# A hand-written order of the attention stage on one Trainium2 core: the repeated period in another order, the last group and its tail in a list of their own

## The reference

```
for gp in 4 head groups, bb in 4 batches:        # a step s = 4*gp + bb
    q, qx, k, v = quantised layernorm(x) @ weights     # row products, 256 rows
    q, qx, k    = layernorm over each head of 128
    4 heads:  softmax(q k^T) v                         # self attention, 256 x 256
    4 heads:  softmax(qx kx^T) vx                      # cross attention, 256 x 64
    y = round to fp8 (concat / smooth);  x += y @ wproj
then x = x + mixture of 32 experts(layernorm(x)), a second attention, a dense ffn
```

## Time and profile before

| | us |
|---|---|
| median of 3 runs | 820.1 (819.15 to 820.65) |
| the profiled execution | 821.01 |
| its span | 819.2 |
| PE busy in the span | 776.4 (95%) |
| PE's weight loads | 669.2 (82%) |
| DVE busy | 642.5 (78%) |
| ACT busy | 538.4 (66%) |
| POOL busy | 495.5 (60%) |
| granted TensorE clock, mean | 0.991 of full |

### The profile page before, as it was taken

How to read it: one execution, slowest core, us unless ns; L and a number is a source line. 1 busy time by engine, 2 the same in 40 slices (tenths; PEclk the granted TensorE clock), 3 DMA queues, 4 the chain that set the end, 5 groups by cost and what they waited for, 6 DMA issues and landing times.

```text
span 819.2 us, 14427 instructions
## 1 busy us (share of the span) xinstructions
PE 776.4 (95%) x4848; PEld 669.2 (82%) x4848; DVE 642.5 (78%) x1509; ACT 538.4 (66%) x1236; POOL 495.5 (60%) x858
## 2 busy tenths in 40 slices
PE   3678999999999999999899999999999999999997
PEld 2467888889888899888778878898888877777787
DVE  6878998989888898889889795766754658886644
ACT  6889878798787987788664555433332267986332
POOL 2698879997699976997856477424210125627410
PEclk9989999999999999999999999999999999999999
DMA  7000120012101030000200322977513000001001
GB/s 248 13 1 1 50 68 1 2 39 60 59 1 34 20 98 6 2 1 2 69 27 14 110 87 56 237 191 255 175 44 99 21 1 14 27 1 39 1 1 52
DMA packets 29224, 45.59 MB, mean 56 GB/s; under 512 B 4128, under 2 KB 18272, under 8 KB 29024
## 3 DMA queue, kind: packets, MB, share of 16 engines
q1 hardware_dynamic: 27760, 41.31, 17.0%
q10 hardware_dynamic: 1392, 3.37, 1.2%
HBM read 43.49 MB, written 1.18 MB: 55 GB/s over the span
## 4 chain that ended last, share of the span: by engine, by line
PE 81%; DVE 6%; ACT 6%; DMA 2%; issue 2%; POOL 2%; SPq 1%; ACTq 0%; DVEq 0%
PE PS L1077 17%; PE PS L937 10%; PE PS L1147 9%; PE PS L1032 6%; PE PS L968 6%; PE PS L1006 6%; PE PS L959 4%; PE PS L1261 3%; PE PS L978 3%; PE PS L989 3%; PE PS L1016 2%; PE PS L1213 2%; DMA l_S<-share 1%; PE PS L1223 1%; PE PS L1229 1%
## 5 line engine op out<-in xcount | busy, mean ns | idle before, releaser
L3240 POOL TENSOR_SCALAR raw<-raw,mvq,rsq 128x128 f32<-128x128 f32 x312 | 194.8, 638 | 1.6
L1077 PE MATMUL PS<-xq,WH 128*128 128x512 f32 x472 | 149.2, 397 | 0.0
L1077 PEld LDWEIGHTS PS<-xq,WH 128*128 128x128 f32 x472 | 86.3, 190 | 17.5 <-issue 1.9
L937 PE MATMUL PS<-WH,xq 128*128 128x256 f32 (+1 forms) x256 | 91.2, 373 | 9.9 <-DVE xq L2102 5.6
L1077 PE MATMUL PS<-xq,WL 128*128 128x512 f32 x236 | 92.9, 393 | 0.0
L937 PE MATMUL PS<-WL,xq 128*128 128x256 f32 (+1 forms) x256 | 83.3, 342 | 0.0
L2202 DVE BATCH_NORM_STATS2 st<-raw 128x6 f32<-128x128 f32 x320 | 75.3, 277 | 9.1 <-ACT raw L1398 7.7
L1147 PE MATMUL PS<-xq,m_hh 128*128 128x256 f32 x384 | 70.3, 283 | 2.0 <-ACT m_hh L1312 1.4
L1032 PE MATMUL PS<-PH,cat 128*128 128x256 f32 x256 | 67.8, 301 | 0.9 <-DVE cat L2102 0.9
L1426 ACT ACTIVATE P<-PS,sm 128x256 f32<-128x256 f32 x128 | 59.9, 483 | 13.1 <-DVE sm L2266 13.0
L1006 PE MATMUL PS<-PT,vr 128*128 128x256 f32 x256 | 66.3, 381 | 1.9 <-ACT kT L1415 1.4
(11 more groups left out here) (316 smaller groups left out, 2120.6 us busy)
## 6 DMA issues: line engine op xcount, KB each, us to landing
wst<-in_wgu SPq DMA_DIRECT2D x24, 256.0 KB, 2.9
wst<-in_wall SPq DMA_DIRECT2D x18, 256.0 KB, 3.1
l_KM<-share SPq DMA_DIRECT2D x9, 384.0 KB, 3.9
dst<-in_wdn SPq DMA_DIRECT2D x24, 128.0 KB, 2.6
wst<-in_wkvx SPq DMA_DIRECT2D x8, 256.0 KB, 3.4
m_pre<-in_wo ACTq DMA_DIRECT2D x1, 2048.0 KB, 11.7
l_KM<-share SPq DMA_DIRECT2D x6, 256.0 KB, 6.5
l_S<-share SPq DMA_DIRECT2D x6, 256.0 KB, 6.0
```

Source lines behind the costliest of these rows:

```text
L937: t = e.matmul(PS[:, b, o:o + n], xq[s][:, k, c * 128:(c + 1) * 128], W[:, k, w0:w0 + n], start=(k == 0 and i == 0), stop=(k == 1 and i == 1))
L1077: t = e.matmul(PS[:, b, :], W[wi][:, gu, k, :], a[:, k, cols], start=(n == 0), stop=(n == 5))
L3240: t = e.tensor_scalar(v, v, mvq[:, par, n, 0:1], rsq[:, par, n:n + 1], ALU.add, ALU.mult)
```

## The change

Only orders change. No operation is added, removed or resized; PE's list has the same 505 calls before and after.

- The period of 20 units is written in another order on PE, ACT and DVE, and nearly the same on POOL, and is now repeated twice (g = 0, 1).
- The third repetition and the regular pattern behind it (`BEGUN`, `ROUND`) are replaced by explicit lists, one for each engine.
- The copies of the next stages' first weights move: `split_gate`, `load_gu(0)` to `load_gu(3)` on ACT are spread over the tail; on POOL `load_p(3, 2)` and `load_p(3, 3)` come before the last two heads of step 14 and not after them, and `zero`, `load_gu`, `load_dn` and `turn_keys` behind step 15 change places.
- `logits(1)` moves behind the last projection. Three waits are written out in `load_gu` and `load_p` that the old lists had beside them.

```
-    for g in range(3):
+    for g in range(2):
         do("scores", 2 + 4 * g, 3)
         do("values", 2 + 4 * g, 0)
         do("turn", 2 + 4 * g, 1)
+        do("p2", 3 + 4 * g, 1)
         do("kx", 1 + g)
-        do("p2", 3 + 4 * g, 1)
+        do("values", 2 + 4 * g, 1)
         do("scores", 2 + 4 * g, 4)
+        do("turn", 2 + 4 * g, 2)
         do("p1", 1 + g, 2, 2)
...
-        do("project", 3 + 4 * g, 0)
-        do("p1", 1 + g, 7, 2)
...
+        do("p1", 1 + g, 7, 0)
+        do("p1", 1 + g, 6, 1)
+        do("scores", 5 + 4 * g, 1)
+        do("scores", 5 + 4 * g, 2)
+        do("p2", 6 + 4 * g, 4)
+        do("p1", 1 + g, 7, 1)
+        do("scores", 5 + 4 * g, 3)
...
-    for n in range(BEGUN, len(units) + 5):
...
+    do("values", 15, 4)
+    do("early", 0, 0)
+    do("project", 15, 0)
+    do("project", 15, 1)
+    do("early", 1, 0)
+    do("project", 15, 2)
+    do("project", 15, 3)
+    do("xs", 2)
+    do("logits", 1)
```

More of the change, by code:

```diff
@@ L313, in attention_order @@
+        do("p1", 2 + g, 1, 1)
+        do("project", 4 + 4 * g, 3)
         do("p2", 7 + 4 * g, 0)
-    units = [(s, k) for s in range(STEPS) for k in range(5)]
-    for n in range(BEGUN, len(units) + 5):
[L316 to L350, removed]
@@ new lines, in attention_order @@
+    do("scores", 10, 3)
+    do("values", 10, 0)
+    do("turn", 10, 1)
+    do("p2", 11, 1)
+    do("kx", 3)
+    do("scores", 10, 4)
+    do("values", 10, 1)
+    do("turn", 10, 2)
+    do("p2", 11, 2)
+    do("p1", 3, 2, 2)
+    do("values", 10, 2)
+    do("turn", 10, 3)
+    do("scores", 11, 0)
+    do("p2", 11, 3)
+    do("p1", 3, 3, 2)
+    do("values", 10, 3)
+    do("scores", 11, 1)
+    do("turn", 10, 4)
+    do("project", 9, 0)
+    do("project", 9, 1)
+    do("p1", 3, 2, 0)
+    do("p1", 3, 3, 0)
@@ new lines, in attention_order @@
+    do("project", 9, 2)
+    do("scores", 11, 2)
+    do("p2", 12, 4)
+    do("scores", 11, 3)
+    do("values", 10, 4)
+    do("turn", 11, 0)
+    do("project", 9, 3)
+    do("p1", 3, 2, 1)
+    do("p1", 3, 3, 1)
+    do("p2", 12, 0)
+    do("values", 11, 0)
+    do("turn", 11, 1)
+    do("p1", 3, 4, 2)
+    do("scores", 11, 4)
+    do("p2", 12, 1)
+    do("values", 11, 1)
+    do("scores", 12, 0)
+    do("turn", 11, 2)
+    do("p2", 12, 2)
+    do("scores", 12, 1)
+    do("values", 11, 2)
+    do("turn", 11, 3)
@@ new lines, in attention_order @@
+    do("p2", 12, 3)
+    do("project", 10, 0)
+    do("p1", 3, 5, 2)
+    do("project", 10, 1)
+    do("p1", 3, 4, 0)
+    do("p1", 3, 5, 0)
+    do("values", 11, 3)
+    do("turn", 11, 4)
+    do("p1", 3, 4, 1)
+    do("project", 10, 2)
+    do("project", 10, 3)
+    do("p1", 3, 5, 1)
+    do("scores", 12, 2)
+    do("p2", 13, 4)
+    do("values", 11, 4)
+    do("scores", 12, 3)
+    do("turn", 12, 0)
+    do("p2", 13, 0)
+    do("kt", 3)
+    do("project", 11, 0)
+    do("values", 12, 0)
+    do("scores", 12, 4)
@@ new lines, in attention_order @@
+    do("turn", 12, 1)
+    do("vx", 3)
+    do("p2", 13, 1)
+    do("p1", 3, 6, 2)
+    do("values", 12, 1)
+    do("turn", 12, 2)
+    do("project", 11, 1)
+    do("p2", 13, 2)
+    do("scores", 13, 0)
+    do("values", 12, 2)
+    do("turn", 12, 3)
+    do("scores", 13, 1)
+    do("p2", 13, 3)
+    do("p1", 3, 7, 2)
+    do("values", 12, 3)
+    do("p1", 3, 6, 0)
+    do("scores", 13, 2)
+    do("turn", 12, 4)
+    do("p1", 3, 7, 0)
+    do("project", 11, 2)
+    do("p1", 3, 6, 1)
+    do("p2", 14, 4)
@@ new lines, in attention_order @@
+    do("values", 12, 4)
+    do("scores", 13, 3)
+    do("turn", 13, 0)
+    do("project", 11, 3)
+    do("p2", 14, 0)
+    do("p1", 3, 7, 1)
+    do("values", 13, 0)
+    do("turn", 13, 1)
+    do("project", 12, 0)
+    do("p2", 14, 1)
+    do("values", 13, 1)
+    do("turn", 13, 2)
+    do("p2", 14, 2)
+    do("scores", 13, 4)
+    do("values", 13, 2)
+    do("turn", 13, 3)
+    do("scores", 14, 0)
+    do("scores", 14, 1)
+    do("project", 12, 1)
+    do("p2", 14, 3)
+    do("values", 13, 3)
@@ new lines, in attention_order @@
+    do("turn", 14, 3)
+    do("scores", 15, 2)
+    do("p2", 15, 3)
+    do("project", 13, 2)
+    do("xs", 0)
+    do("project", 13, 3)
+    do("values", 14, 3)
+    do("turn", 14, 4)
+    do("scores", 15, 3)
+    do("keys")
+    do("values", 14, 4)
+    do("turn", 15, 0)
+    do("scores", 15, 4)
+    do("keys_r")
+    do("values", 15, 0)
+    do("turn", 15, 1)
+    do("logits", 0)
+    do("values", 15, 1)
+    do("turn", 15, 2)
+    do("project", 14, 0)
+    do("values", 15, 2)
+    do("turn", 15, 3)
```

1015 lines of the change are left out of this document (683 added, 332 removed).

## The result

The changed kernel took 812.34 us (median of 4 runs, 811.22 to 814.06) against 820.38 for the kernel before beside it: ratio 0.9909, interval 0.9889 to 0.993, or 8.0 us. A second series of the same kernel gave 813.55 against 820.8 (6 and 24 runs), ratio 0.9921, interval 0.9904 to 0.9939, or 7.3 us.

The account below looks back on a forecast made before the run. PE, busy for 95% of the span, was taken as the bound. Tail -4.3 (-6.1 + 1.5 + 0.3) and period -0.7 + 0.6 gave -4.4 us: 816.6 from the profiled 821.0, 815.7 as median; range 812.8 to 818.9.

Parts of the forecast that it names:

- The stops of the tail, 6.1 us: PE's stops from 385 to 455.4 us: 4.9 idle plus eight restarts of 0.15, the most the tail can give.
- 1.5 us is left here: At xs(0), POOL's xn comes after PE; a remaining stop of 1.5 us, including p2(15, 4).
- DVE's end at position 279.9: DVE finishes begin_q(15) at the latest 279.9 us after the period's beginning, before POOL's root_q and norm_q.
- 0.3 us is left: Turns and values of steps 14 and 15, 2.3 us idle before: longer distances leave 0.3 us.
- The period, -0.7 + 0.6: Repeated period: 0.7 us saved behind cross scores and cross values, 0.6 us lost at places with shorter bank distances.
- The price behind the cross scores: A row product rather than transposes behind the cross scores costs 0.06 us; nine such places vanish, -0.5 us.
- tight place: One of 12 places in the period where a bank is reused sooner; 0 to 0.6 us each, +0.6 us taken.
- So this part moves along with the attention's end: Behind the attention the order is the same and logits(1) only changes sides, so this part neither gains nor loses.
- the one-hot near 1.1 us: PE's wait for the router's one-hot, behind the attention, stays near 1.1 us.
- DVE did not take the tail over: Rival 1: DVE, at 93% in the tail, comes late and only a quarter of 6.1 us is won; 818.5, chance 0.15.
- The new order stalled: Rival 2: banks not yet free stall the period, 0.7 us at each of 12 places gives 823.5; chance 0.08.
- The weight loads: Rival 4: the period itself shortens, its weight loads filling 88.58 of 98.54 us; 2.7 us more, 813.0, chance 0.07.

Follow-up runs that it names:

- pool_late: Changed kernel with three zeroings of KZ ahead of POOL's norm_m(0) instead of one behind it; 814.66 us, ratio 0.9934.
- begin_late: Changed kernel with DVE's maxima(13, 4) put back ahead of the last five steps of begin_q(15); 816.94 us, ratio 0.9946.
- old_list: Kernel before with the new period run twice, its third repetition and rule for the last units left old; 821.32 us, ratio 1.0006.
- logits_back: Changed kernel with logits(1) moved back ahead of the last two projections; 814.59 us, ratio 0.9925.

## Why the prediction was nearly right, and where it was short

- **The stops of the tail, 6.1 us.** Right, and a little low: idle time of 4.89 us gave 6.53. With 0.15 for each of eight restarts 6.1 is explained; the other 0.4 is not idle time, and was not taken apart.
- **"1.5 us is left here", at `xs(0)`.** This is the largest term of the tail that failed. It measured 0 in one profile and 0.7 in the other. The mechanism held (*pool_late*, *begin_late*), the sizes did not: DVE's end at position 279.9 "at the latest" was 278.5, root_q 5.5 us was 4.4, the next norm 7.5 was 6.9; norm_q(15) was 13.1 for my 12.3. The first was a bound, the others single readings of the same step in the old order. I called the sum late by 1.9 "at the latest", and took four fifths of it as the value. The kernel before would have warned me: its sixteen root_q took anything from 4.2 to 6.5 us. The lock on the shared ports, which I cited against root_q, fits its one long instruction in the change (0.62 us, to 392.11, beside a DVE operation with two inputs in SBUF that ends at 392.05) and those of 1.09 and 0.69 in *begin_late*: such meetings make the spread of this chain.
- **"0.3 us is left" at turns and values.** It was 0, in both profiles.
- **The period, -0.7 + 0.6.** The net of -0.1 over 2.7 repetitions was -0.09 a repetition. Both terms were too large. The price behind the cross scores is real (0.057 us with a row product), but only a third of it is saved: six of the eight in two periods paid it before, and of the eight now four have values behind them, which pay 0.056 as well. And no tight place stopped in this profile. The place with the least room had 0.3 us, where I counted 0.14. The stop that does come at times, 0.5 us at `p2(7, 4)`, is POOL's, not a bank's.
- **"So this part moves along with the attention's end", the one-hot near 1.1 us.** Half of it was right, and sharply: at full clock PE waits 1.6 us longer and the one-hot comes at the same time (11.26 and 11.27 us in *before* and *old_list*). The other half failed. I asked only whether logits(1) delays PE, not whom it lets go earlier: DVE's last norm, and with it POOL's products, run 0.84 us earlier against the router, and the one-hot's way becomes 1.3 us shorter. From there to the end the profiled pair saved 1.7 us. Without the move, in *logits_back*, PE waited 3.9 us there at full clock, and the median was 1.0 to 2.3 us above the change's two, which the intervals do not separate.
- **The first wait of the down products** was in no term:
```profile
PE PS L1147 <- ACT m_hh L1312: 1.4, 1, 1.4
```
before, and now
```profile
PE PS L1269 <- DVE m_hl L3321: 0.3, 1, 0.3
```
The wait for m_hh was anything from 0 to 1.6 us over the profiles of this study, with old and new order. What makes it so was not tried, so this part of the 1.7 us is not shown to be the change's.
- **The rivals.** DVE did not take the tail over: of its 124.27 us in 139.76, 89%, none was late. The new order stalled twice in eighteen repetitions, by 0.5, and not by banks. The weight loads went from 88.58 to 88.34 us a period, and the period did not follow their share.

Added up: 0.2 in the periods, 6.5 in the list and 1.7 behind it are 8.4 us; in the second profile 0.2, 5.8 and 2.3, 8.3 us. The medians gave 8.0 and 7.3.

## What to carry to other kernels

A residue at the end of a chain of several engines should be summed from likely values, over all repetitions of a step and not one, with the bounds kept for the range; a sum "at the latest" made a stop of 1.5 us for a chain that arrives 0.14 us early in one profile and 0.6 late in another. When a small step is moved past others, follow who is released by it, down to the phase in which VectorE and GpSimd then meet: here that shifted the one-hot by 0.8 to 2.5 us in the traces, for a step of 1.3, though the medians cannot show it. And an order for one engine is only as good as that of the engine which feeds it: begin_q(15) early alone stopped PE elsewhere, and PE's distances without it lost 2 to 3 us.

## What was unexpected of the hardware

The VectorE operation into m_tmp, 128x128 with two inputs in SBUF, met a GpSimd product of 128x512 and ended 0.15 us after it, in 12 of 12 profiles, so that it took anything from 0.35 to 1.40 us. Such a difference repeats from run to run where the orders fix the phase (1.30 to 1.33 us in four kernels), and changes with an edit elsewhere, as with three GpSimd operations of 0.21 us. The half clock came in front of the one-hot in 7 of the 14 profiles, and made the later wait shorter: by the 1.6 us that it had cost in the old order, by 1.9 in the new.
